# Layer 3 of a four-layer kernel: expert rows that carry their own destination and gate, and units spread over four periods

## The reference

```
xn = layernorm(x)
s = attention_n(xn)
g = silu(ffn_n(xn))
x = x + s * g
```

```
buf[e, loc[t, k]] = x[t]                          # kept choices only
hid = gelu(buf @ W_in[:, :256]) * (buf @ W_in[:, 256:])
out = hid @ W_out
y[t] = sum over k of gate[t, k] * out[e[t, k], loc[t, k]]
```

## Time and profile before

| | |
|---|---|
| time, median of 3 runs | 3296.8 (3285.92 to 3304.26) |
| profiled execution, its own time | 3281.92 |
| its span, first to last instruction | 3280.1 |
| mean granted TensorE clock | 0.896 |
| PE busy | 2875.4 (88%) |
| PE weight loads busy | 1752.0 (53%) |
| DVE, ACT, POOL busy | 1845.2 (56%), 1336.7 (41%), 1417.5 (43%) |

### The profile page before, as it was taken

One profiled execution on the slowest core, in us unless ns is written; L12 is line 12 of the kernel. 1 busy time (PEld: TensorE's weight loads), 2 busy tenths in 40 slices (PEclk: granted clock), 3 DMA queues, 4 the chain that ended last, 5 costly groups with the idle time before them and its releaser, 6 DMA issues. The chain is left out here.

```text
span 3280.1 us, 39191 instructions
## 1 busy us (share of the span) xinstructions
PE 2875.4 (88%) x14056; PEld 1752.0 (53%) x14056; DVE 1845.2 (56%) x3075; ACT 1336.7 (41%) x3264; POOL 1417.5 (43%) x1340
## 2 busy tenths in 40 slices
PE   7897799999999999799999999999698877979727
PEld 3564355555555555355555555444387665767526
DVE  6868577677677776365655655443543534344303
ACT  4452433443443343355555555434512234433202
POOL 3324366677676676176777776000004201011350
PEclk8997899999999999799999999999777678787756
DMA  5451100000000000510000000221122112121110
GB/s 186 154 179 54 50 1 1 1 1 1 1 1 1 1 1 1 124 40 14 1 1 1 1 1 3 76 74 42 40 86 85 39 28 57 33 54 33 44 37 26
DMA packets 160929, 128.90 MB, mean 39 GB/s; under 512 B 97688, under 2 KB 136864, under 8 KB 160224
## 3 DMA queue, kind: packets, MB, share of 16 engines
q1 hardware_dynamic: 148832, 90.13, 9.8%
q0 software_dynamic: 11904, 36.27, 3.5%
HBM read 105.70 MB, written 38.47 MB: 44 GB/s over the span
## 5 line engine op out<-in xcount | busy, mean ns | idle before, releaser
L1491 POOL TENSOR_TENSOR work<-work 128x512 f32<-128x512 f32 x384 | 494.9, 1289 | 319.8 <-DVE work L1483 302.8
L63 PE MATMUL bank<-work 64*128 64x256 f32 (+5 forms) x4384 | 593.6, 354 | 33.0 <-issue 11.4
L2039 POOL TENSOR_SCALAR work<-work 128x256 f32<-128x256 f32 x512 | 465.0, 926 | 240.9 <-DVE work L2030 240.8
L63 PEld LDWEIGHTS bank<-work 64*128 64x128 f32 (+4 forms) x4384 | 413.7, 173 | 256.6 <-issue 145.7
L63 PE MATMUL bank<-weights_odd,normed_channels 128*128 128x512 f32 (+3 forms) x1152 | 524.6, 563 | 23.0 <-DVE work L1483 16.2
L63 PE MATMUL bank<-work,weights_even 32*128 32x128 f32 (+4 forms) x1008 | 310.1, 485 | 95.4 <-issue 61.4
L2024 ACT ACTIVATE work<-bank,work 128x256 f32<-128x256 f32 x512 | 236.0, 473 | 195.0 <-DVE work L2010 195.0
L1483 DVE TENSOR_TENSOR work<-bank,work 128x512 f32<-128x512 f32 x360 | 245.4, 686 | 109.9 <-PE bank L63 106.5
L63 PEld LDWEIGHTS bank<-weights_odd,normed_channels 128*128 128x128 f32 x1152 | 183.6, 195 | 161.1 <-issue 80.2
L63 PEld LDWEIGHTS bank<-work,weights_even 32*128 32x128 f32 (+4 forms) x1008 | 132.7, 189 | 229.7 <-issue 185.1
L2010 DVE TENSOR_REDUCE work<-bank 128x2 f32<-128x512 f32 x256 | 164.9, 686 | 132.3 <-PE bank L63 132.3
(11 more groups left out here) (315 smaller groups left out, 4493.8 us busy)
## 6 DMA issues: line engine op xcount, KB each, us to landing
work<-gate_rows_L SPq DMA_DIRECT2D x64, 256.0 KB, 3.1
filter_matrices<-in_L_filters SPq DMA_DIRECT2D x24, 512.0 KB, 8.1
work<-filter_matrices SPq DMA_DIRECT2D x16, 768.0 KB, 4.3
expert_rows_in<-in_zeros SPq DMA_DIRECT2D x8, 640.0 KB, 11.6
weights_odd<-expert_rows_in SPq DMA_DIRECT2D x40, 128.0 KB
expert_rows_out<-weights_odd SPq DMA_DIRECT2D x40, 128.0 KB
weights_even<-expert_rows_in SPq DMA_DIRECT2D x20, 128.0 KB
expert_rows_out<-weights_even SPq DMA_DIRECT2D x20, 128.0 KB
```

Source lines behind the costliest of these rows:

```text
L63: return pe.matmul(out, lhsT, rhs, start=first, stop=last, skip_group_check=True)
L1491: gp.tensor_tensor(self.sum_of(p), self.sum_of(p), self.product_of(p), ALU.add).then_inc(s["l1_add"], 1)
L2039: gp.tensor_scalar(p[:, c], p[:, c], self.sums(n, half, i), None, ALU.mult).then_inc(s["l2_p"], 1)
```

## The change

Four things are done, all in layer 3.

1. **Notes.** A row in DRAM is 132 floats wide (`L3_ROW`): 128 channels and four notes (the row of the token for its second choice, its first expert, the difference of the two gates, the second gate). The notes come from five more DVE operations at the end of routing; the scatter waits for the whole of routing, and before each group POOL copies the notes into the staged rows. Empty slots are prefilled from an input `L3_empty` with a destination of their own behind the tokens' rows; that fill, and zeroes for the rows of results, are copied while layer 2 starts.
2. **Results go to their tokens' rows.** For each unit DVE computes from the notes the destination and the gate (`vector_notes`, four small operations), ACT copies the result with the gate as scale (two operations of 128 columns instead of one of 256), and POOL scatters it (two indirect transfers for each unit) to `token_rows_out`, which has one row for each choice and token. `sync_result` is gone.
3. **Loaded in order.** The 64 gathers and both scalings are gone. SP loads 16 blocks of 256 KB in order when the last scatters have landed, and the joins stand at slots 22 to 36 of the last period.
4. **Order of work.** Periods run over slots 4 to 41 (4 to 39 in the last). Units are 12, 12, 12 and 4. U and W of a period are computed in slots 37 to 40 of the period before (the first ones ahead of all periods), on PE and on ACT alike. For that the inversion runs earlier: two steps a slot at first, done by slot 25, loaded from slot 27 on.

```diff
-L3_PERIODS = (48, 48, 48, 42)
+L3_BEGIN, L3_PERIODS = 4, (42, 42, 42, 40)
-L3_UNITS_OF = (14, 13, 13, 0)
-L3_JOINS = (7, 12, 17, 22, 27, 32, 36, 38)
+L3_UNITS_OF = (12, 12, 12, 4)
+L3_JOINS = (22, 24, 26, 28, 30, 32, 34, 36)
+L3_NOTE = 4
+L3_ROW = P + L3_NOTE
...
 def load(self, sp, on):
+        for i in range(self.EMPTY_PARTS):
+            r = slice(i * L3_SLOTS // self.EMPTY_PARTS, (i + 1) * L3_SLOTS // self.EMPTY_PARTS)
+            sp.dma_start(self.x_rows[r, :], ins["L3_empty"][r, :]).then_inc(s["l3_small"], 16)
+        for at in range(0, 2 * TOKENS, ZERO_ROWS):
+            n = min(ZERO_ROWS, 2 * TOKENS - at)
+            sp.dma_start(self.y_rows[at:at + n, :], ins["zeros"][0:n, :]).then_inc(s["l3_small"], 16)
...
 def vector_route(self, v, on):
+        on.wait_ge(done, at + 10)
+        v.tensor_tensor(by_expert(r.tmp), by_expert(r.first), r.weight(), ALU.mult).then_inc(done, 1)
+        v.tensor_copy(self.note[:, :, 0], self.second_row).then_inc(done, 1)
+        yield
+        on.wait_ge(done, at + 11)
+        v.tensor_reduce(self.note[:, :, 1], by_expert(r.tmp), AX.X, ALU.add).then_inc(done, 1)
+        v.tensor_tensor(self.note[:, :, 2], self.gate[0], self.gate[1], ALU.subtract).then_inc(done, 1)
+        v.tensor_copy(self.note[:, :, 3], self.gate[1]).then_inc(done, 1)
+        yield
...
 def gpsimd_scatter(self, gp, on, g):
-        on.wait_ge(s["zeroed"], self.k.ZEROED)
-        on.wait_ge(s["route"], self.router.at + self.SLOTS_KNOWN)
+        on.wait_ge(s["l3_small"], self.SMALL)
+        on.wait_ge(s["route"], self.router.at + self.router.steps[self.router.nth])
         self.moe_done(on, "moe_act", MOE_ACT, ("stage", g))
+        gp.tensor_copy(self.stage[g % 4][:, :, P:], self.note[:, TPG * g:TPG * (g + 1), :]).then_inc(s["l3_noted"], 1)
+        on.wait_ge(s["l3_noted"], g + 1)
...
+    def vector_notes(self, v, on, n):
+        s, x, done = self.k.sem, self.place(n), self.k.sem["l3_notes"]
+        first, to, gate, at = self.is_first[n % 4], self.to_row[n % 4], self.row_gate[n % 4], len(NOTES) * n
+        self.landed(on, f"places_landed{n % 3}", n // 3 + 1)
+        if n >= 4:
+            self.moe_done(on, "moe_act", MOE_ACT, ("y", n - 4))
+            self.scattered(on, n - 4)
+        v.tensor_scalar(first, x[:, :, P + 1], float(EXPERTS - n // L3_PER_EXPERT), None, ALU.is_equal).then_inc(done, 1)
+        on.wait_ge(done, at + 1)
+        v.scalar_tensor_tensor(out=to, in0=first, scalar=-float(TOKENS), in1=x[:, :, P], op0=ALU.mult, op1=ALU.add).then_inc(done, 1)
+        v.tensor_tensor(gate, first, x[:, :, P + 2], ALU.mult).then_inc(done, 1)
+        on.wait_ge(done, at + 3)
+        v.tensor_tensor(gate, gate, x[:, :, P + 3], ALU.add).then_inc(done, 1)
+
+    def scattered(self, on, n):
+        self.landed(on, f"rows_moved{2 + n % 2}", 2 * 2 * TPG + 2 * (n // 2 + 1))
+
+    def gpsimd_results(self, gp, on, n):
         self.moe_done(on, "moe_act", MOE_ACT, ("y", n))
+        on.wait_ge(self.k.sem["l3_notes"], len(NOTES) * (n + 1))
+        for i in range(L3_WIDTH // P):
+            to = bass.IndirectOffsetOnAxis(self.to_row[n % 4][:, i:i + 1], 0)
+            gp.indirect_dma_start(self.y_rows[:, :], to, self.place_y[n % 2][:, i * P:(i + 1) * P],
+                                  None).then_inc(self.k.sem[f"rows_moved{2 + n % 2}"], 16)
...
 def scalar_down(self, a, on, n):
-        self.landed(on, f"results_stored{n % 2}", n // 2)
-        a.activation(self.place_y[n % 2], self.b_ya[unit_set(n)][:, 0:L3_WIDTH], ACT.Copy).then_inc(self.k.sem["moe_act"], 1)
+        on.wait_ge(self.k.sem["l3_notes"], len(NOTES) * (n + 1))
+        if n >= 2:
+            self.scattered(on, n - 2)
+        for i in range(L3_WIDTH // P):
+            c = slice(i * P, (i + 1) * P)
+            last = a.activation(self.place_y[n % 2][:, c], self.b_ya[unit_set(n)][:, c], ACT.Copy, scale=self.row_gate[n % 4][:, i:i + 1])
+        last.then_inc(self.k.sem["moe_act"], 1)
...
+    def sync_rows(self, sp, on, g):
+        sem, at = self.row_signal(g)
+        for n in (L3_UNITS - 2, L3_UNITS - 1):
+            self.scattered(on, n)
         self.done(on, "l3_rec_mm", REC_MM, QUARTERS - 2, ("score", PAIRS - 1))
         for which in range(2):
+            first = which * TOKENS + g * GW
+            src = self.y_rows[first:first + GW, :].rearrange("(i p) d -> p i d", p=P)
+            sp.dma_start(tiles(self.rows[g][which]), src).then_inc(sem, 16)
...
 def tensor(self, pe, on):
+        for step in range(len(UW)):
+            self.tensor_uw(pe, on, 0, step // 2, "uw"[step % 2])
         for quarter in range(QUARTERS):
-            for slot in range(L3_PERIODS[quarter]):
-                if slot < 4:
-                    self.tensor_uw(pe, on, quarter, slot // 2, "uw"[slot % 2])
+            for slot in range(L3_BEGIN, L3_PERIODS[quarter]):
...
                 if quarter + 1 < QUARTERS:
+                    if 0 <= slot - self.UW_FIRST < len(UW):
+                        step = slot - self.UW_FIRST
+                        self.tensor_uw(pe, on, quarter + 1, step // 2, "uw"[step % 2])
-                elif (g := join_due(slot, 1)) is not None:
+                elif (g := join_due(slot, 0)) is not None:
                     self.tensor_join(pe, on, g)
...
+    UW_FIRST = 37
...
+    def inverted(quarter, slot):
+        if slot < 26:
+            return 2 if slot < (15 if quarter == 0 else 5) else 1
+        return int(slot >= 32)
...
 def gpsimd(self, gp, on):
-        for n in range(L3_UNITS):
-            self.gpsimd_gated(gp, on, n)
-        for g in range(GROUPS):
-            self.gpsimd_gather(gp, on, g)
+        for n in range(L3_UNITS + 1):
+            if n < L3_UNITS:
+                self.gpsimd_gated(gp, on, n)
+            if n > 0:
+                self.gpsimd_results(gp, on, n - 1)
...
 def sync(self, sp, on):
-                    self.sync_result(sp, on, n)
...
                 if slot == self.INVERTED:
+                    if quarter + 1 < QUARTERS:
+                        self.sync_inverses(sp, on, quarter + 1)
+                    if quarter + 2 < QUARTERS:
+                        self.sync_triangles(sp, on, quarter + 2)
+        for g in range(GROUPS):
+            self.sync_rows(sp, on, g)
+
+    INVERTED = 27
```

More of the change, by code:

```diff
@@ L4 @@
 from contextlib import ExitStack
+from itertools import chain
 F32, I32 = mybir.dt.float32, mybir.dt.int32
@@ L2336, in last_unit @@
 def last_unit(q, which):
-    return sum(L3_UNITS_OF[:q]) + (L3_FIRST_SET if which == 0 else L3_UNITS_OF[q]) - 1
+    return sum(L3_UNITS_OF[:q]) + (min(L3_FIRST_SET, L3_UNITS_OF[q]) if which == 0 else L3_UNITS_OF[q]) - 1
 def events(parts):
-    return tuple((what, unit_due(q, slot, lag)) for q in range(QUARTERS) for slot in range(L3_PERIODS[q]) for what, lag in parts
+    return tuple((what, unit_due(q, slot, lag)) for q in range(QUARTERS) for slot in range(L3_BEGIN, L3_PERIODS[q]) for what, lag in parts
                  if unit_due(q, slot, lag) is not None)
@@ L2352, in joins @@
 def joins(parts):
-    return tuple((what, join_due(slot, lag)) for slot in range(L3_PERIODS[-1]) for what, lag in parts
+    return tuple((what, join_due(slot, lag)) for slot in range(L3_BEGIN, L3_PERIODS[-1]) for what, lag in parts
                  if join_due(slot, lag) is not None)
@@ L2359 @@
 MOE_MM = BY_GROUP("stage") + events((("y", 3), ("x", 0), ("a", 1), ("g", 1))) + BY_GROUP("join")
-MOE_ACT = BY_GROUP("stage") + events((("y", 3), ("x", 0), ("gelu", 1), ("second", 1))) + joins((("scale", 0), ("silu", 2)))
+MOE_ACT = BY_GROUP("stage") + events((("y", 3), ("x", 0), ("gelu", 1), ("second", 1))) + joins((("silu", 1),))
 MOE_POOL = events((("gated", 1),))
-MOE_DVE = joins((("scale", 0), ("mixed", 3)))
+MOE_DVE = tuple(("mixed", g) for g in range(GROUPS))
+NOTES = ("first", "to", "part", "gate")
 def four(m):
@@ L2832, in gates_of @@
-    def gates_of(self, which, g):
-        return self.gate[which][:, TPG * g:TPG * (g + 1)].unsqueeze(2).to_broadcast([P, TPG, P])
-    def scalar_scale(self, a, on, g):
-        self.gathered(on, g)
-        on.wait_ge(self.k.sem["route"], self.router.at + self.router.steps[self.router.nth])
-        for i in range(TPG):
-            x, t = self.rows[g][1][:, i * P:(i + 1) * P], TPG * g + i
-            last = a.activation(x, x, ACT.Copy, scale=self.gate[1][:, t:t + 1])
-        last.then_inc(self.k.sem["moe_act"], 1)
@@ L3556, in vector @@
             pass
+        invert = chain.from_iterable(self.vector_invert(v, on, quarter) for quarter in range(1, QUARTERS))
         for quarter in range(QUARTERS):
-            invert = self.vector_invert(v, on, quarter + 1) if quarter + 1 < QUARTERS else iter(())
-            for slot in range(L3_PERIODS[quarter]):
-                c, step = divmod(slot - 4, 3)
+            for slot in range(L3_BEGIN, L3_PERIODS[quarter]):
+                c, step = divmod(slot - L3_BEGIN, 3)
                 if 0 <= c < L3_CHUNKS:
@@ L3614, in sync @@
         self.sync_inverses(sp, on, 0)
```

(6 more changed lines are left out.)

124 lines of the change are left out of this document (59 added, 65 removed).

## The result

The changed kernel takes 3159.8 us, the median of four runs (3147.8 to 3167.6). Beside it the kernel before takes 3291.4 (3284.7 to 3304.3): ratio 0.9593, 95% interval 0.9547 to 0.9638, faster by about 4%. 3157 was predicted. The profiled execution takes 3162.0, its span is 3160.2, the mean granted clock 0.913 (before 0.896).

The account below looks back on a forecast made before the run. PE was held by low-clock U/W and tails and by 77 us of starvation beneath gathers. From 3281.9 us, -155 for the periods and +15 for the scatter gave 3142, with the median's 14.9 offset 3157; range 3105 to 3215.

Parts of the forecast that it names:

- The rival that the shortage isn't the gathers': U and W of the last period stay slow for another reason: +75 us, 3232 us; chance 0.08.
- The rival of 5 us for each unit: Result scatters of two transfers halt PE, 40 units pay; at 5 us each the time is 3357; chance 0.05.
- Heads and mix 80: Heads and mix of three periods, 28 + 29 + 29 us, less 6 because the last inversion steps leave them.
- new stretches 60: Slots 37 to 41, three periods: U, W and one unit, 20 us each (15 to 29), for 225 before.
- Recurrences 226: Three recurrence windows of 74 + 76 + 61 us, plus 15 for inversion steps moved into them.
- the early inverse steps': Last seven inversion steps move from heads into the recurrence, before operations it waits for: 5 us each period, bounds 0 and 20.
- Last period 99: Last period with four more units, higher clock, no scalings, a wait of 4 at the first join: 99 us, bounds 90 to 112.
- Inverses from slot 27, queues, notes, scaled copies: nothing: Later inverse loads, SP queues and small operations for each unit cost nothing; notes, copies and result scatters up to 5 us.
- The scatter: 0 + 15: Scatter after routing: early shortage gone -10, ACT's fifth copy waits +10, shortage beneath 40 transfers taken at a third, +15 us.
- the full shortage at +45: Rival: the scatter's unbroken run starves PE fully, +45 us for +15, 3187 us; chance 0.17.
- Filling the new tensors: nothing: Copies of 9.6 MB more when layer 2 starts, taken at no cost to PE.
- From the profiled execution to the median: +14.9: The median was taken to lie 14.9 us above the profiled execution, as before: 3142 becomes 3157 us.

Follow-up runs that it names:

- the last experiment: Kernel before, with two fills of the product buffer on POOL ahead of every group of eight gathers but the first: 3225.8 us against 3290.0, ratio 0.9820.
- the run with U and W in place: Changed kernel, with U and W of a quarter built ahead of slot 4 of its own period again: 3200.2 us, ratio 0.9734.
- the paused kernel: Changed kernel, with six fills on POOL ahead of every group of eight scatters but the first: 3130.5 us, ratio 0.9503.
- the third series: Kernel before unchanged 3294.5 us, changed kernel unchanged 3171.3, changed kernel with staging from slot 21 and pauses between scatters 3125.1; kernel before beside them 3300.5.
- three edits of it: Kernel before, with pauses between gathers 3192.3 us, gathers replaced by plain transfers from POOL 3192.8, or from SP 3194.1; kernel before beside them 3193.7.

## Why the prediction came out right, and what in it was wrong

**The shortage of 77 us is the gathers'.** Shown. The reading of the earlier trace rows held: a pause between groups of eight is enough to be rid of a shortage, on scatters and on gathers, with their number and data unchanged. Alone it brings 64 us of the change's 132. Whether it is the pause itself or the lower mean rate that comes with it, no run tells. The rival that the shortage isn't the gathers' falls with the last experiment.

**Gathers gone, and the result scatters that replace them.** No shortage beside runs of two transfers: 471 and 465 matmuls in 79 and 78 us. The rival of 5 us for each unit didn't come.

**Heads and mix 80, new stretches 60: measured 26 + 24 + 22 = 72 and 32 + 30 + 25 = 87, together 159 for 140.** Where one ends and the other begins is partly a choice of the windows, so they are read together: 19 us too few. A count shows why. In the earlier trace rows POOL's 14 products of a period lie 7, 3 and 4 in recurrence, heads and tail. I kept 7 and 3 and put one unit in the new stretch: that is 11, and the period has 12. At the sum's own 4.5 to 6.5 us for a unit the missing one is 13 to 20 us over three periods. The groups of PE by shape, changed kernel, 2803 to 2835 us:

```profile
L64 PE MATMUL bank<-weights_even,work 128*128 128x32 f32 x64 | 8.6, 297 | 0.0
L64 PE MATMUL bank<-weights_odd 128*128 128x256 f32 x23 | 8.1, 515 | 0.0
L64 PE MATMUL bank<-weights_odd 128*128 128x128 f32 x24 | 3.4, 283 | 0.8 <-POOL weights_odd L2858 0.8
```

The layer has 320 of each of the last two shapes for its 40 units, 8 for each, so this stretch of 32 us holds three units beside U and W, and the heads before it two. PE is busy 26.4 of the 32: the stretch is full of work, not of waits. (32 and 30 us also lie outside the 15 to 29 that the prediction had set as its sign.) That the move pays is shown by the run with U and W in place: 41 us over three periods.

**Recurrences 226: measured 79 + 78 + 64 = 221.** DVE is busy 61 and 57 us in the first two, as forecast, and PE idle 10 in each. Only 1 us of these is a wait for DVE, 8 are one for ACT (L3183), so DVE did not set the pace. How much of that idle time is the early inverse steps' (+5 each in the sum) wasn't tried alone.

**Last period 99: measured 82.2**, below the lower bound of 90. PE is busy 69.4 us, less than the 74.5 of the earlier trace rows although four units came in; the clock is 0.93 and 0.92 instead of 0.69. I had let it rise without giving it a price. The wait of 4 us at the first join didn't come either. All from the inverses to the end: 481 where 485 was worked out. The 19 us too few and the 17 too many cancel.

**Inverses from slot 27, queues, notes, scaled copies: nothing.** No wait of PE for diagonal matrices after the first; agrees.

**The scatter: 0 + 15. Wrong: +40.8, and it is the term that failed.** What was worked out as a rival, the full shortage at +45, happened: 39 matmuls in 30 us are 13 in 10 us, and under 20 was to be its sign. Two parts are seen. ACT's copy of the fifth group waits for the first group's rows (ACT's timeline):

```profile
2533.24 0.60 ACT L2733 ACTIVATE weights_odd<-bank 128x512 f32<-128x512 f32 x1 [17.55 <-DMA noted_rows_in<-weights_odd,expert_slots]
```

PE stands for 11.6 us behind it, where the sum had 10 and set it off against the early shortage, which did go. And the copy of the notes between the groups, 0.24 us, refills nothing. I had taken a third of 45 for it, between the ends, though the nearest row (a pause of about 3 us) spoke for a pause ten times as long. At the pace of the paused kernel (206 in 30 us) the 39 matmuls take 6 us: 24 lost. The pauses bring back some 29 us of the time.

These parts come to -10 + 11.6 + 24 = 26, not 40.8. Another 6 us lie ahead of the first transfer, which starts at 2521.9 where 2516 was forecast. The run with U and W in place is the same program up to there; it starts at 2514.1 and has its inverses at 2671.8, only 33.7 us late. What differs is the clock in layer 3's opening, here the changed kernel and then that run:

```profile
2280.00:2450.00 170.00, 139.94 (x662) 100.71 (x661) 74.36 (x156) 63.81 (x90) 0.00 (x0) 0.67 0.18 58
2280.00:2450.00 170.00, 138.93 (x703) 100.29 (x702) 75.67 (x159) 68.00 (x97) 0.00 (x0) 0.75 0.17 58
```

So some 7 of the 40.8 us belong to this one execution and not to the change. Of the rest some 5 lie behind the shortage: from 2579 to 2655 the changed kernel does 439 matmuls in 76 us at a clock of 0.66, and the paused one, from 2559 to 2614, 339 in 55 at 0.82. What is left, under 5, is not taken apart.

**Filling the new tensors: nothing.** Agrees. Nor do the ordered loads at the end hold PE: 46.2 busy of 49 us (3078 to 3127) at a DMA share of 0.37, twice that of any shortage. The rule of the Trainium skill ("DMA: Bandwidth & Descriptors", "Queues, rings and completion order"), that a DMA engine takes turns between its queues, would have it otherwise as I had applied it to PE's supply; the trace disagrees here too.

**From the profiled execution to the median: +14.9. Wrong: -2.2.** A single execution lies anywhere among the others (in the third series the changed kernel's profiled one was some 18 us above its median). In the profiled execution's terms the sum was 3142 and the trace gives 3162; this offset hid it. That the forecast came within 3 us of the time is luck: two errors of 17 to 19 us cancelled in the periods, and the 26 us too few for the scatter met 17 us too many in this offset and 6 in the periods (160.7 us less where 155 was worked out).

## What to carry to other kernels

When PE slows without a semaphore wait while POOL issues indirect transfers, look at how long POOL's run is, not at the bytes alone: break it every eight transfers with some 2 us of fills, and measure that before redesigning the transfers, since here it brought half of the gain. When a stage gets faster, look at what stands behind it in an idle-looking queue: a fill of 3.5 us at the end of POOL's scatters took back 13 us. And work of PE put beside other work, not alone, had the higher clock here (0.84 instead of 0.57 for U and W); price a stretch at the clock it will have, in the last period too. Last, time kernels that are to be compared in one series: the kernel before differed by 3% between two of them on one chip.

## What the runs showed of the hardware

- **The starvation depends on something outside the kernel.** The kernel before took 3268 to 3308 us in three of the series, on three chips, and 3181 to 3211 in 25 runs of the second, on the chip of the first. In the second, three edits of it show no shortage in their scatters, which are those of the kernel before. Their gathers are edited, so that for its own gathers only its time speaks. What differs between the series is open. The changed kernel itself wasn't run in the second; with a fill ahead of each scatter it gained 2.5% there, and with pauses it gained 5.0% in the first. So, it seems, part of the gain exists only where the starvation does.
- **It isn't a late instruction packet, as far as the records go.** The trace has a queue of instruction packets. Queues in the 77 us of gathers, the kernel before (first) and the same with pauses:

```profile
q0 software_dynamic: 1771, 3.61, 17.9%
q14 instruction: 1, 0.01, 0.0%
```

```profile
q0 software_dynamic: 1611, 3.28, 15.2%
q1 hardware_dynamic: 576, 1.05, 3.7%
q8 instruction: 3, 0.05, 0.2%
```

  No packet of queue 8 in the first, three in the second. But one such packet (16 KB) comes for each 130 or so matmuls (90 to 160, mostly 115 to 145) in both kernels, and so it is here: one at 3103.8, the next at 3200.5, with some 130 matmuls between. They keep step with the matmuls, slow or fast, and the one of 3103.8 had landed 1.4 us later, ahead of the shortage. What I called a stock that isn't refilled is therefore not shown to be the supply from memory; that some store between it and PE is starved remains an inference.
